# A third transpose bank in a relative-position attention kernel, and transposes sent ahead of scores

## The reference

```
q, k, v = heads of (xn @ W.T + b)
idx   = clip(pos_k - pos_q, -20, 20) + 20          # 41 distances
attn  = softmax((q . k + q . rel_k[idx]) / sqrt(8))
x_att = attn @ v + sum over keys of attn * rel_v[idx]
out   = x_att @ Wo.T + bo
```

## Time and profile before

| | |
|---|---|
| median of 3 runs | 2473.31 us (2469.48 to 2473.86) |
| the profiled execution | 2466.72 us, its span 2464.9 us |
| busy: PE, DVE, ACT, POOL | 2128.0, 1864.7, 1619.9, 1030.4 us |
| exponentials of `attend` (L818) | 1024, the first at 100.4 us, the last at 1551.5 us |
| granted TensorE clock, mean | 0.961 |

### The profile page before, as it was taken

One profiled execution on the slowest core, in us unless ns is written; L12 is line 12 of the kernel. 1 busy time (PEld: TensorE's weight loads), 2 busy tenths in 40 slices (PEclk: granted clock), 3 DMA queues, 4 the chain that ended last, 5 costly groups with the idle time before them and its releaser, 6 DMA issues. The chain is left out here.

```text
span 2464.9 us, 77225 instructions
## 1 busy us (share of the span) xinstructions
PE 2128.0 (86%) x27816; PEld 1444.4 (59%) x27816; DVE 1864.7 (76%) x4151; ACT 1619.9 (66%) x4178; POOL 1030.4 (42%) x1270
## 2 busy tenths in 40 slices
PE   3388888888888888888888888599999978999999
PEld 1266566666666666666666666356666645666665
DVE  1388888888888888888888889367676756877777
ACT  2288888888888888888888878367777752323222
POOL 4246655655656656556655554200000003333332
PEclk7699999999999999999999999789999998999999
DMA  3355655555655655555555554200100110010110
GB/s 101 104 123 130 149 137 120 148 134 121 149 130 127 147 136 129 140 134 128 144 134 125 136 119 83 46 23 26 39 26 26 38 61 26 30 35 26 32 32 18
DMA packets 571232, 228.63 MB, mean 93 GB/s; under 512 B 465590, under 2 KB 543030, under 8 KB 566326
## 3 DMA queue, kind: packets, MB, share of 16 engines
q1 hardware_dynamic: 570934, 224.63, 36.8%
HBM read 129.61 MB, written 94.90 MB: 91 GB/s over the span
## 5 line engine op out<-in xcount | busy, mean ns | idle before, releaser
L818 ACT ACTIVATE a_probs<-a_bank_s,a_neg_max 128x512 f32<-128x512 f32 x1024 | 695.0, 685 | 134.0 <-DVE a_neg_max L679 131.0
L679 DVE TENSOR_REDUCE a_neg_max<-a_bank_s 128x2 f32<-128x1024 f32 x512 | 627.1, 1225 | 55.6 <-DVE a_bank_s L644 1.9
L481 PE MATMUL a_bank_pt<-a_ident,a_probs 128*128 128x128 f32 x4096 | 588.2, 284 | 64.8 <-ACT a_feat_t L830 42.9
L481 PEld LDWEIGHTS a_bank_pt<-a_ident,a_probs 128*128 128x128 f32 x4096 | 444.1, 143 | 201.0 <-issue 67.5
L792 ACT ACTIVATE a_probs_t<-a_bank_pt 128x512 f32<-128x512 f32 x512 | 306.0, 598 | 138.7 <-PE a_bank_pt L481 136.9
L661 DVE COPY a_probs_t<-a_bank_pt 128x512 f32<-128x512 f32 x512 | 349.7, 683 | 26.9 <-PE a_bank_pt L481 21.9
L502 PE MATMUL a_bank_o<-a_probs_t,a_v 128*32 128x128 f32 x8192 | 285.4, 281 | 1.4 <-issue 0.2
L644 DVE TENSOR_TENSOR a_bank_s<-a_bank_s,a_win 128x144 f32<-128x144 f32 (+2 forms) x640 | 161.3, 271 | 148.2 <-PE a_bank_s L469 145.3
L1537 ACT ACTIVATE e_gate<-e_bank_g 128x512 f32<-128x512 f32 x144 | 85.9, 597 | 273.9 <-PE e_bank_g L1476 273.9
L502 PEld LDWEIGHTS a_bank_o<-a_probs_t,a_v 128*32 128x32 f32 x8192 | 215.0, 112 | 58.1 <-issue 39.6
L937 POOL TENSOR_TENSOR a_win<-a_raw,a_band 128x1152 f32<-128x1152 f32 x64 | 168.9, 2639 | 105.2 <-issue 73.8
(11 more groups left out here) (163 smaller groups left out, 3489.7 us busy)
## 6 DMA issues: line engine op xcount, KB each, us to landing
scr_probs<-a_probs SPq DMA_DIRECT2D x512, 72.0 KB, 2.4
a_raw<-scr_qr SPq DMA_DIRECT2D x256, 96.0 KB
scr_qr<-a_qr SPq DMA_DIRECT2D x64, 320.0 KB, 3.6
a_feat<-scr_probs SPq DMA_DIRECT2D x256, 78.0 KB, 2.4
scr_parts<-a_sp SPq DMA_DIRECT2D x144, 128.0 KB, 2.4
a_left<-scr_probs SPq DMA_DIRECT2D x256, 64.0 KB, 2.5
a_q<-scr_parts SPq DMA_DIRECT2D x32, 192.0 KB
a_k<-scr_parts SPq DMA_DIRECT2D x32, 192.0 KB
```

What stands on the lines that cost most here:

```text
L481: ins = nc.tensor.transpose(b_pt[bank_of(job)][:, 0, t * P:(t + 1) * P], probs[(u - 1) % 4][:, j, MAX_REL + t * P:MAX_REL + (t + 1) * P], ...
L679: nc.vector.tensor_reduce(neg_max[:, 2 * pair:2 * pair + 2], b_s[:, 2 * pair:2 * pair + 2, :], AX.X, ALU.max, negate=True).then_inc(max_ok, 1)
L818: nc.scalar.activation(probs[u % 4][:, j, MAX_REL:MAX_REL + S], b_s[:, j, :], ACT.Exp, bias=neg_max[:, j:j + 1], accum_out=sums[:, t, PLAC ...
```

## The change

Four edits, all in `attend`:

1. `b_pt` has three banks instead of two. The bank of a job is its place in the list modulo 3, and there is a semaphore `pt_ev` for each.
2. The bank `b_w` is gone. The feature products of query blocks 0, 1 and 2 are added by TensorE to the attended values in `b_o` (no start flag). Those of block 3 come when `b_o` has already been copied out; they are a new job, `WEIGHED` at u = 5, in a bank of `b_pt`.
3. VectorE adds that job's 128 by 128 numbers at u = 5, where it added 128 by 512 at u = 6. `scale` on GpSimd waits for that addition and for `o_ev`.
4. In each half TensorE issues the transposes of the pair first (in pair 1 behind `attended`), and the new scores after them. Before, the scores came first. The warm-up products of the first entry go from u = 3 to the end of u = 2.

```diff
+PT_BANKS = 3
+WEIGHED = (5, "weigh", 0)
-JOBS += [(u, "features", n) for u in range(0, UNITS, 4) for n in range(2)] + [(9, "out", n) for n in range(2)]
+JOBS += [(u, "features", n) for u in range(0, UNITS, 4) for n in range(2)] + [WEIGHED] + [(9, "out", n) for n in range(2)]
...
 def bank_of(job):
-    return JOBS.index(job) % 2
+    return JOBS.index(job) % PT_BANKS
...
-        b_pt = [ps(f"pt{n}") for n in range(2)]
-        b_o, b_w = ps("o"), ps("w")
+        b_pt = [ps(f"pt{n}") for n in range(PT_BANKS)]
+        b_o = ps("o")
...
-                first = hh == 0
+                first = u == 0
...
-                if t == 0:
-                    need(pe, w_ev, b, 1, 0)
+                apart = t == NT - 1
+                if apart:
+                    bank_free(pe, b, WEIGHED)
+                out = b_pt[bank_of(WEIGHED)][:, 0, 0:P] if apart else b_o[:, 0, t * P:(t + 1) * P]
                 for c in range(FC):
-                    ins = nc.tensor.matmul(b_w[:, 0, t * P:(t + 1) * P], feat_w[:, c, :],
-                                           feat_t[:, c, :] if c < FC - 1 else last_t[:, t, :],
-                                           start=c == 0, stop=c == FC - 1)
-                ins.then_inc(w_ps, 1)
+                    ins = nc.tensor.matmul(out, feat_w[:, c, :], feat_t[:, c, :] if c < FC - 1 else last_t[:, t, :],
+                                           start=apart and c == 0, stop=c == FC - 1, skip_group_check=True)
+                ins.then_inc(pt_ps if apart else w_ps, 1)
...
                     for pair in ((0, 1), (2, 3)):
-                        if not tail:
-                            scores(b, u, pair, s)
                         if pair[0]:
                             if u > 2 and not tail:
                                 attended(b, u - 3, s)
...
                         for j in pair:
                             if (u and not tail) or (u == 0 and not first):
                                 transpose(b, u, j)
+                        if not tail:
+                            scores(b, u, pair, s)
+                    if first and u == 2:
+                        warm_up(nc, b_o[:, 0, 0:P], ident[:], WARM)
...
-                    if u == 6 and not first:
-                        v.wait_ge(w_ps, b * NT)
+                    if u == 5 and not first:
+                        job_done(v, b, WEIGHED)
                         v.wait_ge(o_ev, b)
-                        nc.vector.tensor_tensor(o_sb[:], o_sb[:], b_w[:, 0, :].rearrange("p (t q) -> p t q", q=P),
-                                                ALU.add).then_inc(w_ev, 1)
+                        nc.vector.tensor_tensor(o_sb[:, NT - 1, :], o_sb[:, NT - 1, :], b_pt[bank_of(WEIGHED)][:, 0, 0:P],
+                                                ALU.add).then_inc(pt_ev[bank_of(WEIGHED)], 1)
```

More of the change, by code:

```diff
@@ L79 @@
 OF_ROW_BEFORE = [(0, "probs", j) for j in range(NJ)] + [(u, "features", n) for u in (0, 4) for n in range(2)]
-OF_ROW_BEFORE += [(9, "out", n) for n in range(2)]
+OF_ROW_BEFORE += [WEIGHED] + [(9, "out", n) for n in range(2)]
 def of_row(b):
@@ L97, in count @@
     def count(jobs):
-        return sum(bank is None or JOBS.index(x) % 2 == bank for x in jobs)
+        return sum(bank is None or bank_of(x) == bank for x in jobs)
     earlier = JOBS[:JOBS.index(job)]
@@ L193, in attend @@
         s_ps, max_ok, exp_ok = sem("s_ps"), sem("max_ok"), sem("exp_ok")
-        pt_ps, pt_ev = sem("pt_ps"), [sem("pt_ev0"), sem("pt_ev1")]
-        av_ps, w_ps, o_ev, w_ev = sem("av_ps"), sem("w_ps"), sem("o_ev"), sem("w_ev")
+        pt_ps, pt_ev = sem("pt_ps"), [sem(f"pt_ev{n}") for n in range(PT_BANKS)]
+        av_ps, w_ps, o_ev = sem("av_ps"), sem("w_ps"), sem("o_ev")
         p_out = [sem(f"p_out{k}") for k in range(4)]
@@ L560, in row @@
                                 attended(b, u - 3, s)
-                                if first and u == 3:
-                                    warm_up(nc, b_w[:, 0, 0:P], ident[:], WARM)
                             elif u < 3 and not first:
@@ L697, in row @@
                         job_done(v, b, job)
+                        if t == 0 and not first:
+                            job_done(v, b, WEIGHED)
                         if t == 0:
-                            need(v, w_ps, b, NT, 0)
                             need(v, att_ok, b, 1, 0)
@@ L828, in row @@
                         job_done(act, b, job)
-                        need(act, w_ps, b, NT, u // 4 - 2)
+                        if u != 8:
+                            need(act, w_ps, b, NT - 1, {0: -1, 4: 0, 12: 1}[u])
+                        elif not first:
+                            job_done(act, b, WEIGHED)
                         nc.scalar.activation(feat_t[:], b_pt[bank_of(job)][:, 0, :].rearrange("p (c q) -> p c q", q=P),
@@ L989, in scale @@
             def scale(b):
-                g.wait_ge(w_ev, b)
+                g.wait_ge(o_ev, b)
+                job_read(g, b, WEIGHED)
                 g.wait_ge(spread_ok, b * NT)
```

## The result

The changed kernel takes 2864.37 us (median of 4 runs, 2851.38 to 2884.00) against 2471.39 us; the ratio is 1.160, interval 1.153 to 1.167. The forecast was 2736 us with a range up to 2800: right in sign, 128 us short. The profiled execution took 2851.38 us, 384.7 us more than the one of before.

What follows compares the result with a forecast made beforehand. No engine is full; handovers between three nearly full ones decide. Entry: 106.2 us plus 3.6 for the clock, 109.8; thirteen entries + 230, last two + 22, first + 11: + 263 on 2466.72, 2730 profiled, 2736 median, range 2640 to 2800.

Steps and rivals of the forecast that it cites:

- the chain: Behind extra jobs: DVE waits for scores, scores for transpose 1, it for ScalarE, ScalarE for DVE; 4.88 or 4.78 us.
- the term for the clock: Each entry: TensorE's idling lowers its clock to 1.2 GHz; three falls taken, 3.6 us, from an open none to nine.
- rival "slower by more: the clock": Whole kernel: nine clock falls an entry instead of three, 108 us more, 2844 us; 8 in 100.
- 7 units lose their addition: Last two entries: no preparing jobs, so 7 units escape the added time; + 11 us each, 22.
- features: Second half of 4 units with a feature job: pair 1's addition to the next pair 0's takes 4.88 us.
- output product: Second half of unit 9: pair 1's addition to the next pair 0's takes 4.78 us, held by ScalarE's reading.
- one extra job: Second half of units 3, 6, 13: transpose 1 waits for DVE's copy of transpose 3; 3.52 us.
- `WEIGHED`: Second half of unit 5: transpose 1 waits until VectorE has read this job; 4.43 us.
- most first halves: In 14 units, pair 0's addition to pair 1's takes 2.39 us instead of 2.16, attended values now between the scores.
- Unit 2's second half and unit 3's first: Attended values in unit 3 wait for ScalarE's copy of `b_o`; 2.16 + 4.26, together 6.42 us.
- What was at zero: Feature products in `b_o`, VectorE's smaller addition and GpSimd's earlier scaling: no cost or gain, 0 us.
- rival "faster": Whole kernel: third bank removes waits, scores still come before DVE is free; 105 us less, 2368; 3 in 100.

Runs made afterwards that it cites:

- fill_idle: Changed kernel with TensorE repeating feature transposes, qr products and transpose 0 where it would idle, waits untouched: 2760.43 us, ratio 1.117.
- bank_only: Changed kernel with the scores of each half sent first again, the rest of the change kept: 2445.16 us, ratio 0.990.
- ahead_small: ahead with the 18 query and key loads of each entry from the third on cut to one row of 64 numbers: 2367.69 us, ratio 0.959.
- ahead_before: Kernel before, two banks, with TensorE's extra jobs sent behind the next unit's scores of pair 0: 2470.6 us, ratio 0.9995.
- bank_split: bank_only with the count of qr stores split in two, one for each qr buffer: 2444.52 us, ratio 0.989.
- ahead: bank_split with TensorE's extra jobs at a unit's end sent behind the next unit's scores of pair 0: 2438.68 us, ratio 0.987.
- order_only: Kernel before, two banks, with only the order changed, transposes sent before scores in each half: 3275.2 us, ratio 1.326.

## Why the prediction was wrong

The mechanism was right, and so was the chain. The step that failed is the term for the clock: "I take three falls, 3.6 us". The 13 entries of the changed kernel show what should have stood there. Taking an entry's time at 1.2 GHz from its granted clock as above (13 us for the entry of 109.99 us, 44 us for the one of 122.64 us), a straight line through the 13 lengths starts at 106.1 us with no time at the lower level and rises by 0.346 us for each us of it; the points lie close to it (correlation 0.98, the start good to about 0.6 us). The start is the chain with the clock up, which the prediction had at 106.2. The mean entry spends 28.6 us at the lower level, so the clock costs 28.6 x 0.346 = 9.9 us of it, where the sum has 3.6. Both factors were too small: 6.4 falls instead of three, and 1.5 us each instead of 1.2.

The line alone doesn't say which is cause and which effect, since a longer entry also gives TensorE more idle time. fill_idle says it: it spends 4.5 us an entry at the lower level; the 24.1 us less, at 0.346, are 8.3 us. It gained 7.0 with the filling to pay.

The sentence before the three falls had nine (10.8 us) as its upper end, and the rival "slower by more: the clock", with nine falls, gave 2844 us with 8 in 100; the measured 2864 us lies 20 us above it. The reason given for three ("the longest idle stretches now give one each") rested on no row. The rows left the number open. In the earlier trace rows a qr job was followed by the lower level, and TensorE had waited 1.42 us before it:

```profile
709.33 0.90 PE L451 MATMUL a_bank_pt<-a_relx,a_t 64*128 64x320 f32 x4 [1.42 <-DVE a_probs_t L661]
```

But the earlier trace rows has 52 waits of that kind in 13 entries, and they came with only 11 falls.

The account in the profiled execution, forecast against measured:

- 13 entries: 13 x (109.8 - 92.1) = 230 against 310.9 us, 81 more. The clock term alone is (9.9 - 3.6) x 13 = 82 of it.
- The two last entries, the end of the block and the second block: + 22 against 1131.97 - 1076.67 = + 55 us (2849.6 - 1717.63 and 2464.9 - 1388.23), 33 more. Of the 55 us, 3 lie behind the last exponential; some 13 are the clock by the slope above (42 us at the lower level against 3); about 39 are the chain, 19 an entry, where the forecast's 11 an entry had 3.6 for the clock and so about 7 for the chain. This was a second wrong step: "7 units lose their addition". The banks are numbered by place in the list, and missing jobs leave their place empty, so the hold doesn't go away. Unit 10 of the 15th entry has no qr job:

```profile
1785.71 0.68 DVE L664 COPY a_probs_t<-a_bank_pt 128x512 f32<-128x512 f32 x1
...
1786.44 1.09 PE L483 MATMUL a_bank_pt<-a_ident,a_probs 128*128 128x128 f32 x8 [2.38 <-DVE a_probs_t L664]
...
1787.46 0.32 PE L471 MATMUL a_bank_s<-a_kl,a_q 48*32 48x236 bf16 x8
...
1787.95 0.32 DVE L647 TENSOR_TENSOR a_bank_s<-a_bank_s,a_win 128x144 f32<-128x144 f32 x1 [1.56 <-PE a_bank_s L471]
```

  Transpose 0 waits for DVE's copy of the last transpose before it, which has the same bank, and the scores wait with it: DVE idles 1.56 us where I had it at work without a pause. That the empty places are the cause is read from the wait and the list; no run numbered the banks otherwise.
- The first entry: + 11 against 109.49 - 90.72 = + 18.8 us, 8 more. The clock is about 5 of the 18.8 (23 us at the lower level against 9.5), hardly more than the 3.6 in the forecast; the rest was not looked into.

Term by term, with the row "fill" of the table, where the clock is up: features 4.74 to 4.79 (forecast 4.88), output product 4.53 (4.78), one extra job 3.37 to 3.52 (3.52), `WEIGHED` 4.13 (4.43: its addition takes 0.23 us, and TensorE starts transpose 0 meanwhile), most first halves 2.38 to 2.46 (2.39). qr is lengthened by the filling; in the changed kernel it is 4.65 and 4.82 in units 10 and 11 (4.78). Unit 2's second half and unit 3's first, 2.16 + 4.26 = 6.42, are 2.64 + 3.66 = 6.30. One first half was missed: unit 8's is 3.16 with and without fill. It is the same kind of hold, by a job of ScalarE at the end of unit 7 that I had not placed in the chain. In the entry shown above:

```profile
259.63 0.63 ACT L745 ACTIVATE a_sp<-a_t 128x512 bf16<-128x512 f32 x1
...
260.15 0.72 ACT L771 ACTIVATE a_t<-a_t,a_left_less 128x512 f32<-128x512 f32 x1
...
260.77 0.59 ACT L795 ACTIVATE a_probs_t<-a_bank_pt 128x512 f32<-128x512 f32 x1
...
261.41 0.66 PE L483 MATMUL a_bank_pt<-a_ident,a_probs 128*128 128x128 f32 x4 [1.01 <-ACT a_probs_t L795]
```

With three banks, transpose 3 of a unit has the bank of transpose 0. ScalarE copies transpose 0 only behind its two preparing writes, transpose 3 waits 1.01 us for that copy, and the scores of pair 1 stand behind it. That the chain's total came out within about 0.1 us is in part luck: this half was 0.8 too short in the sum, and other terms were up to 0.3 too long.

What was at zero did no harm: the products in `b_o` and the smaller addition together cost no more than the third bank gives (bank_only, which has all three, is faster than the kernel before). The rival "faster" had one true part: waits for banks can go, and with the scores first the whole is worth 26 us (bank_only). With the scores queued behind the rotation it gave a loss.

## What to carry to other kernels

In an in-order queue, put first what depends on least: scores that needed only old exponentials were made to wait for everything that a transpose's bank waits for. Before moving an instruction behind another, follow the other's waits through the engine that must release them, and see whether that engine in turn waits for the instruction moved; then each microsecond added to that circle is paid. And where a change makes idle stretches in TensorE, price the lower clock for every one of them, not for some: all nine at 1.2 us would have given 10.8 of the measured 9.9 us, three gave 3.6.

## What the runs showed that I had not expected

- Keeping TensorE busy with repeated work made the changed kernel 104 us faster (clock of the entries 0.88 to 0.98), although the filling lengthened some halves.
- Five versions with the scores first all end at 90 to 92 us an entry; only ahead_small, with transfers cut, is lower (85.4): `before` 92.1, ahead_before 91.8, bank_only 90.5, bank_split 90.8, ahead 90.3.
- The changed kernel's four runs span 33 us, those of before 5 us, and the slowest of the four has the lowest clock (0.883 against 0.890 to 0.896). A low clock alone does not do it: the two runs of order_only, at 0.86, lie 3 us apart.
